# First attention of a macaron block pair: side work in smaller pieces per slot, and score products on 64-row halves with two key copies

## What is computed

```python
    def _L0_attn_ref(x, Wq, bq, Wk, bk, Wv, bv, Wo, bo):
        ...
        q = x @ Wq + bq
        k = x @ Wk + bk
        v = x @ Wv + bv
        ...
        scores = jnp.einsum('bghnd,bhsd->bghns', q, k)
        attn = jax.nn.softmax(scores / SCALE, axis=-1)
        out = jnp.einsum('bghns,bhsd->bghnd', attn, v)
        out = out.transpose(0, 3, 1, 2, 4).reshape(B, N, NUM_HEADS * HEAD_DIM)
        return out @ Wo + bo
...
    x = x + 0.5 * _L0_ffn_ref(_layernorm(x, axis=-1), ...)
    x = x + _L0_attn_ref(_layernorm(x, axis=-1), ...)
    x = x + 0.5 * _L0_ffn_ref(_layernorm(x, axis=-1), ...)
```

## Time and profile before

| | us |
|---|---|
| median of three runs | 1548.53 |
| profiled execution | 1547.1 |
| its span | 1545.2 |
| PE busy (matmul) | 1458.9 |
| DVE busy | 1103.2 |
| ACT busy | 956.2 |
| POOL busy | 581.6 |

### The profile page before, as it was taken

The page is one execution under the profiler, slowest core; times in us unless marked ns, Lnnn a source line. Parts: engine busy times, 40 slices in busy tenths (PEclk is TensorE's granted clock), DMA queues, the critical chain, the costliest instruction groups (busy, mean ns, idle before and its releaser), DMA issues.

```text
span 1545.2 us, 27899 instructions
## 1 busy us (share of the span) xinstructions
PE 1458.9 (94%) x9950; PEld 1189.4 (77%) x9950; DVE 1103.2 (71%) x2377; ACT 956.2 (62%) x1710; POOL 581.6 (38%) x551
## 2 busy tenths in 40 slices
PE   6999999889999999899999998999989999989998
PEld 6788888765555555488888887799977777769998
DVE  4766766777888888466766765477768888866765
ACT  6455555446666666655555556577736666658886
POOL 4466666500000000006666664477720111126664
PEclk9999999999999999999999998899999999999999
DMA  6000000000000000000000004000000000000000
GB/s 173 0 1 1 1 1 1 1 1 1 1 1 1 1 2 1 1 1 1 1 1 1 0 1 166 1 2 1 2 1 1 1 2 1 2 2 1 15 15 29
DMA packets 13320, 16.88 MB, mean 11 GB/s; under 512 B 768, under 2 KB 10496, under 8 KB 12928
## 3 DMA queue, kind: packets, MB, share of 16 engines
q1 hardware_dynamic: 13184, 15.11, 3.1%
HBM read 13.01 MB, written 2.10 MB: 10 GB/s over the span
## 4 chain that ended last, share of the span: by engine, by line
PE 78%; DVE 9%; ACT 8%; issue 4%; DMA 1%; POOL 0%; DVEq 0%; SPq 0%; POOLq 0%; ACTq 0%
PE PS L604 20%; PE PS L632 10%; PE PS L1738 9%; PE PS L1751 8%; PE PS L761 3%; PE PS L740 3%; PE PS L748 3%; ACT AR L855 2%; PE PS L718 2%; PE PS L1108 2%; PE PS L1112 2%; PE PS L1083 2%; PE PS L1065 1%; PE PS L1093 1%; PE PS L1132 1%
## 5 line engine op out<-in xcount | busy, mean ns | idle before, releaser
L542 POOL TENSOR_TENSOR RR<-AR,RR 128x512 fp32r<-128x512 f32 x150 | 193.9, 1293 | 516.1 <-ACT RR L565 516.1
L579 ACT ACTIVATE AR<-PS 128x512 f32<-128x512 f32 x224 | 134.0, 598 | 197.3 <-PE PS L604 196.1
L521 DVE TENSOR_TENSOR AR<-AR,PS 128x512 f32<-128x512 f32 x224 | 153.7, 686 | 132.4 <-PE PS L604 132.3
L855 ACT ACTIVATE AR<-PS 128x512 f32<-128x512 f32 x256 | 149.5, 600 | 98.1 <-PE PS L748 96.7
L924 DVE TENSOR_REDUCE AR<-PS 128x2 f32<-128x512 f32 x256 | 173.4, 686 | 47.3 <-PE PS L740 45.6
L604 PE MATMUL PS<-XHI,WG 128*128 128x512 f32 x448 | 175.8, 392 | 0.0
L604 PE MATMUL PS<-XHI,WU 128*128 128x512 f32 x448 | 174.6, 390 | 0.2
L525 DVE TENSOR_TENSOR AR<-AR,PS 128x512 f32<-128x512 f32 x224 | 153.8, 687 | 8.0 <-POOL RR L542 0.3
L1738 PE MATMUL PS<-XHI,SL 128*128 128x256 f32 x576 | 133.8, 287 | 2.5 <-DVE XTR L1904 1.4
L1738 PE MATMUL PS<-XLO,SL 128*128 128x256 f32 x576 | 133.0, 286 | 1.5 <-DVE XTR L1904 1.3
L1828 ACT ACTIVATE PS<-PS 128x1024 f32<-128x1024 f32 x96 | 96.8, 1009 | 55.1 <-PE PS L1738 54.9
(11 more groups left out here) (299 smaller groups left out, 3466.7 us busy)
## 6 DMA issues: line engine op xcount, KB each, us to landing
X<-in_x SPq DMA_DIRECT2D x4, 512.0 KB, 6.4
RAWZ<-in_zone_up SPq DMA_DIRECT2D x8, 256.0 KB, 4.8
RAWZ<-in_zone_down SPq DMA_DIRECT2D x8, 256.0 KB, 5.0
out_x<-X SPq DMA_DIRECT2D x4, 512.0 KB, 3.2
AR<-in_w SPq DMA_DIRECT2D x1, 1792.0 KB, 11.6
XT<-in_w SPq DMA_DIRECT2D x1, 1608.0 KB, 8.8
XT<-in_sel SPq DMA_DIRECT2D x1, 896.0 KB, 7.0
SM<-in_small SPq DMA_DIRECT2D x1, 857.5 KB, 6.8
```

Of the source, the lines that this page charges most:

```text
L521: v.tensor_tensor(PRD[:, m % 2, :], SIL[:, m % 2, :], bank(2 + m % 2), ALU.mult).then_inc(S.prod, 1)
L542: g.tensor_tensor(HL[k % 3], GAT[:, m % 2, :], HH[k % 3].bitcast(F32), ALU.subtract).then_inc(S.h_lo, 1)
L579: act.activation(SIL[:, m % 2, :], bank(m % 2), ACT.Silu).then_inc(S.silu, 1)
L855: act.activation(PT[:, g % 2, k, 2 * jp:2 * jp + 2, :], bank(2 + m % 2).rearrange("p (j q) -> p j q", j=2), ACT.Exp, scale=SC0).then_inc(S ...
```

## The change

*Key copies.* `KS0` keeps two copies (o = 0, 1). Copy o is zero on the groups g with g % 2 != o, by the new mask `ODD[:, o]` (sum of mask columns o and o + 2, made once). A score product takes only 64 partitions, `half_rows(h)`: 0 to 63 hold groups 0 and 1, 64 to 127 groups 2 and 3. `scores(b, m)` takes h = m // 4 % 2 and j = m % 4, both copies, so the second half of the queries is needed from place 2 on, not 4. `scores_t(b, m)` goes through the groups in the ORDER 0, 2, 1, 3. With the lead of 4, at any slot `scores` and `scores_t` are on different halves and in different banks. The address of the maxima and the layout of the outputs follow.

*Pieces.* `values` is called per half of the keys (k), four products each, in two adjacent slots; `queries` becomes `query`, one product per slot; `turn(i - 1, 1)` and `maxima` are halved over two slots; slots are dealt anew on PE (in the diff), ACT and DVE. On ACT `keys` goes from slots 0, 1 to 3, 4, `query` from 3 to 6 to 5, 6, 8, 9, and `rounded` from 7, 8 to 7, 10. On DVE `vals` goes from slot 2 to 4, `key_stacks` from 3, 4 to 5, 7, `normalise(i - 1, 1)` from 5 to 6, `stacks` from 8, 9 to 9, 13, and `normalise` of half 0 from slot 13 to slot 1 of the next step.

```diff
-            def queries(b, half):
-                if half:
+            def query(b, j):
+                half = j // 2
+                if j == 2:
                     pe.wait_ge(S.kx, b + 1)
                     pe.wait_ge(S.v, b + 1)
...
             def scores(b, m):
-                k, j, gp = m // 8, m // 2 % 4, m % 2
+                k, h, j = m // 8, m // 4 % 2, m % 4
...
-                if m in (0, 4):
-                    pe.wait_ge(S.qs, 2 * b + m // 4 + 1)
+                if m in (0, 2):
+                    pe.wait_ge(S.qs, 2 * b + m // 2 + 1)
                 wait(pe, S.smax, NS0 * b + m - 1)
-                pe.matmul(bank(m % 2), QS0[b % 3][:, j * SEQ + k * P:j * SEQ + (k + 1) * P], KS0[b % 3][:, 2 * gp:2 * gp + 2, :],
-                          start=True, stop=True).then_inc(S.s_pe, 1)
+                pe.matmul(bank(m % 2), QS0[b % 3][half_rows(h), j * SEQ + k * P:j * SEQ + (k + 1) * P],
+                          KS0[b % 3][half_rows(h), :, :], start=True, stop=True).then_inc(S.s_pe, 1)
...
-                g, k, jp = m // 4, m // 2 % 2, m % 2
-                pe.matmul(bank(2 + m % 2), KS0[b % 3][:, g, k * P:(k + 1) * P], QS0[b % 3][:, jp * 512:(jp + 1) * 512],
+                g, k, jp = ORDER[m // 4], m // 2 % 2, m % 2
+                rows = half_rows(g // 2)
+                pe.matmul(bank(2 + m % 2), KS0[b % 3][rows, g % 2, k * P:(k + 1) * P], QS0[b % 3][rows, jp * 512:(jp + 1) * 512],
                           start=True, stop=True).then_inc(S.st_pe, 1)
 
-            def values(b, g):
-                pe.wait_ge(S.exp, NS0 * b + 4 * g + 4)
+            def values(b, g, k):
+                pe.wait_ge(S.exp, NS0 * b + 4 * g + 2 * k + 2)
...
-                    if m == 0 and far:
+                    if m < 2 and done:
+                        values(i - 1, 3, m)
+                    if m == 2 and far:
                         key_value(i + 2)
-                    if m == 1 and done:
-                        values(i - 1, 3)
-                    if m == 1 and far:
-                        queries(i + 2, 0)
-                    if m == 3 and far:
-                        queries(i + 2, 1)
-                    if m == 4 and done:
-                        turn(i - 1, 1)
-                    if m in (5, 9) and now:
-                        values(i, m // 4 - 1)
-                    if m == 7 and done:
+                    if m in (3, 4) and far:
+                        query(i + 2, m - 3)
+                    if m in (4, 5) and done:
+                        turn(i - 1, 1, m - 4)
+                    if m in (5, 6) and now:
+                        values(i, 0, m - 5)
+                    if m in (6, 7) and far:
+                        query(i + 2, m - 4)
+                    if m == 8 and done:
                         back(i - 1)
-                    if m == 10 and done:
+                    if m in (9, 10) and now:
+                        values(i, 1, m - 9)
+                    if m == 11 and done:
                         project_out(i - 1)
                     if m == 12 and now:
-                        turn(i, 0)
-                    if m == 13 and next_:
-                        maxima(i + 1)
-                    if m == 13 and now:
-                        values(i, 2)
+                        turn(i, 0, 0)
+                        turn(i, 0, 1)
+                    if m in (13, 14) and next_:
+                        maxima(i + 1, m - 13)
+                    if m in (14, 15) and now:
+                        values(i, 2, m - 14)
...
-                for g in (2 * part, 2 * part + 1):
-                    last = v.tensor_scalar(KS0[b % 3][:, g, :], KSF0, T.masks[:, 2 + g:3 + g], None, ALU.mult)
+                ins = v.tensor_scalar(KS0[b % 3][:, part, :], KSF0, ODD[:, part:part + 1], None, ALU.mult)
```

More of the change, by code:

```diff
@@ L680, in program @@
         QH0 = XHI[:, 3072:4096]
-        KS0 = [XLO[:, u * 1024:(u + 1) * 1024].rearrange("p (g k) -> p g k", g=4) for u in range(3)]
+        KS0 = [XLO[:, u * 512:(u + 1) * 512].rearrange("p (o k) -> p o k", o=2) for u in range(3)]
         KH0 = XLO[:, 3072:3328]
@@ L711, in key_value, with maxima @@
                 last.then_inc(S.kv, 1)
-            def queries(b, half):
-                if half:
+            def query(b, j):
+                half = j // 2
+                if j == 2:
                     pe.wait_ge(S.kx, b + 1)
                     pe.wait_ge(S.v, b + 1)
[L717 to L722, removed]
+                ins = pe.matmul(bank(5 - half)[:, j % 2 * SEQ:(j % 2 + 1) * SEQ], T.wqs[:, j * P:(j + 1) * P], x_of(b),
+                                start=True, stop=True)
+                if j % 2:
+                    ins.then_inc(S.q, 1)
+            def maxima(b, half):
                 pe.wait_ge(S.mm, b + 1)
@@ L725, in maxima @@
                 for k in range(2):
-                    for j in range(4):
+                    for j in (2 * half, 2 * half + 1):
                         last = pe.transpose(bank(4, 2)[:, j * SEQ + k * P:j * SEQ + (k + 1) * P],
@@ L758, in values, with turn @@
                 o = bank(6 + g // 2)
[L759 to L765, removed]
-                pe.wait_ge(S.os, 2 * b + half + 1)
[L767 to L771, removed]
+                for j in range(4):
+                    last = pe.matmul(o[32 * j:32 * j + 32, g % 2 * SEQ:(g % 2 + 1) * SEQ], VA3[:, b % 3, k, ORDER[g], :],
+                                     PT[:, g % 2, k, j, :], start=(k == 0), stop=(k == 1), skip_group_check=True)
+                if k:
+                    last.then_inc(S.av, 1)
+            def turn(b, half, k):
+                pe.wait_ge(S.os, 2 * b + half + 1)
+                for g in range(2):
+                    at = half * 512 + g * SEQ + k * P
+                    last = pe.transpose(bank(6 + half)[:, (k * 2 + g) * P:(k * 2 + g + 1) * P], OS[:, at:at + P], ident)
+                if k:
+                    last.then_inc(S.ot, 1)
             def back(b):
@@ L893, in a0_dve @@
             rchain, mchain, kchain = Chain(v, S.r_chain), Chain(v, S.m_chain), Chain(v, S.k_chain)
+            kchain.link(v.tensor_tensor(ODD, T.masks[:, 2:4], T.masks[:, 4:6], ALU.add))
             def vals(b):
@@ L928, in maxima @@
                 v.wait_ge(S.smax, NS0 * (b + 1))
-                wait(v, S.mt, b)
+                wait(v, S.mt, 2 * b)
                 if b == 0:
@@ L969, in step @@
                         smax(b, s)
-                    if m == 2 and far:
+                    if m == 1 and done:
+                        normalise(i - 1, 0)
+                    if m == 4 and far:
                         vals(i + 2)
-                    if m in (3, 4) and far:
-                        key_stacks(i + 2, m - 3)
-                    if m == 5 and done:
+                    if m in (5, 7) and far:
+                        key_stacks(i + 2, m // 7)
+                    if m == 6 and done:
                         normalise(i - 1, 1)
-                    if m in (8, 9) and far:
-                        stacks(i + 2, m - 8)
+                    if m == 9 and far:
+                        stacks(i + 2, 0)
                     if m == 11 and next_:
@@ L981, in step @@
                         add(i - 1)
-                    if m == 13 and now:
-                        normalise(i, 0)
+                    if m == 13 and far:
+                        stacks(i + 2, 1)
                     if m in (14, 15) and next_:
```

35 lines of the change are left out of this document (22 added, 13 removed).

## The result

The changed kernel takes 1574.1 us (four runs, 1571.6 to 1576.5) against 1547.7 before; the ratio is 1.0171 with a 95% interval of 1.0147 to 1.0195. It is slower by 1.7%. I had forecast 1533.5 and the range 1515 to 1565, so the sign and the range are wrong. The profiled execution took 1576.5 us, with a span of 1574.6, 29.4 us more than before.

The account below looks back on a forecast made before the run. PE was taken to bound the first attention, with 17.1 us of work and 3.3 of waits per 20.44 us step. A new step of 18.6 + 0.6 = 19.2 us gave -15 us in all: 1533.5 us, range 1515 to 1565.

Parts of the forecast that it names:

- PE's floor before and after: PE's own work in one step of the first attention: 17.1 us before the change, 18.6 us after.
- the price of a pair (0.43): Two score products on opposite halves: load 0.10, one stream 0.23, drain 0.10, so 0.43 us against 0.46 before.
- half a block (0.57): Half a block of values on PE: 0.57 us, 1.00 less two groups of 0.22, eight a step.
- a change of the array's division by rows as by columns: Switching PE between row halves and other tilings costs the same as by columns: 0.19 against 0.20 us.
- the two rivals on concurrency: Score pairs: halves not streaming together (0.66 us, total 1576, chance 0.14), or only weight loads in a row (0.54, 1549, 0.15).
- The waits of `key_value` and of the second queries: PE's waits for DVE's shifts (slot 0) and the values' bias (slot 3) both go: -1.55 us a step.
- DVE's fewer key copies: Two of four masked copies go, 0.6 us of DVE a step; worth nothing on the path.
- part (a): Fewer waits in a step: two go, -1.55 us; a slot-by-slot walk found 0.3 left, 0.6 taken.
- The waits move: Rival: DVE's reduce-shift chain or ACT in slots 8 to 10 holds PE as long as now; 1569 at worst, chance 0.14.
- the sum (e): Step 19.2 us: thirteen steps -16, start +1.6, first and last but one -0.5 each, last +0.5; together -15 us.
- the rival without concurrency: The halves of a score pair do not stream together: pair 0.66 us, +27 us, total 1576, chance 0.14.
- part (c): Opposite halves: a pair of score products streams together on PE and costs 0.43 us against 0.46 before.

Follow-up runs that it names:

- e4: The changed kernel with the second half of the query stacks on DVE in slot 12, ahead of the addition, not slot 13: 1526.3 us, ratio 0.9853.
- e10: e8 with three keep-busy products instead of one after each score product in the start: 1588.7 us, one execution.
- e5: The changed kernel with full 128-row score products, four key copies and the second query stack in slot 12: 1526.8 us, ratio 0.9869 against the kernel before.
- e1: The changed kernel with full 128-row score products and four key copies again, keeping the new dealing of slots: 1547.0 us, ratio 1.0001 against the kernel before.
- e7: The changed kernel with five full keep-busy products inside PE's wait for the second query stack, from the third batch on: 1563.6 us, ratio 1.0112.
- e2: The kernel before with only the halves (two key copies, 64-row products, new group order), old dealing of slots: 1567 to 1600 us in four runs.
- e6: e4 with the start's full keep-busy product replaced by a second 64-row product on the opposite half, in 20 slots: 1537.5 us, ratio 0.9936.
- e8: e4 with both score products of each slot on the same 64 rows: 1585.0 us, ratio 1.0274; two more executions took 1834.3 and 1835.7 us.
- e9: e4 with 128-row products from own key copies for the first pass of batch 0 and second pass of batch 15: 1520.5 us, ratio 0.9828.

## Why the prediction was wrong

*Right.* PE's floor before and after, the price of a pair (0.43), of half a block (0.57), of a change of the array's division by rows as by columns, and the two rivals on concurrency as not true: e4's step is 18.64 for a floor of 18.6, e10's 21.95 for 22.2. The waits of `key_value` and of the second queries went as said. That DVE's fewer key copies were worth nothing on the path fits e5, where DVE waits 0.39 us for PE between its four copies and the second half of the stacks; no run took the copies alone.

*Wrong, first:* the step that failed in the waits is part (a), the walk through the new step. I took DVE's chain of slots 12 to 15 with the stacks in slot 13 and compared its end with what waits for the two shifts. I did not ask who waits for the stacks themselves. The diff has it: `if m in (0, 2)`, where it was `(0, 4)`, and place 2 stands in slot 14. The wait of 1.5 to 1.7 us made the waits of a step 1.25 us where I took 0.6; 13 x 0.65 = 8 us, and a forecast of 1542 with all else as it was. The rival "The waits move" (0.14) was nearest in kind, but it looked at the shifts and at ACT. e4 shows the cause: with the stacks one slot earlier the step is 18.64.

*Wrong, second and larger:* in the sum (e), a cost put at nothing without a reason. Every stretch was taken at the clock of before. The earlier trace rows showed 1.00 and I read it as given. The change put half-array products in the place of full ones and left an idle wait between them; then the clock fell, at the start for 47.8 us, in the steps and at the end. The start alone was +16.6 where (e) had +1.6, the first full step +5.1 for -0.5, the last +5.7 for +0.5, and the low stretches of the thirteen steps were 10.2 where the sum had none. That the time is near the 1576 of the rival without concurrency is chance: its mechanism is refuted by the starts of the pairs.

*Wrong, and of no weight:* two of the signs. The product behind a pair was to start some 0.33 us after it; by part (c) itself it is 0.43, and that was measured. ACT's wait for L755 was to fall well below 5.8 us; it was 6.2 (500 to 520 us), and 5.0 in the step of e4.

*What stays open.* Which property of PE's work lets the clock fall was not separated. Full products with the same wait kept it (e1), and in the changed kernel the low stretches of the steps went when the wait was taken away (e4) or filled (e7). But the wait is not needed: halves lost the clock in e2 with no wait over 0.84 us, in e6 in a last step that kept it in e4, and in e4's own start. Pairs on both halves in the start lost it too (e6), so neither the missing half nor the drains alone explain it. Where the low stretches begin differs between executions (e4, e8).

## What to carry to other kernels

When a change makes matmuls smaller or makes TensorE wait, check the granted clock stretch by stretch before and after, and price a stall with the clock that it may cost: here one stall of 1.5 to 1.7 us a step was worth 48 us. When an operation is moved and its consumer is moved too, look for the new consumer of each moved result, by name, not only for those that waited before. Here halves of the array gave 0.5 us a step where both were busy (e4 against e5); where one stood alone, at the ends of the pipeline, full products were the better choice (e9 against e4). When a small difference hangs on the clock, look at several executions: one kernel here took 1585 or 1835 us.

## What was new of the hardware

Products on opposite 64-row halves start within 0.003 to 0.004 us of each other in most pairs (232 of 256 in the changed kernel) and take the time of one; their weight loads start together as well. A pair stood 0.43 us before the next piece in another division, against 0.66 on one half.

The lower level of the clock can last under full load: in the profiled execution of e8 the granted clock was 0.50 for 621 us with PE busy 99.9% of it, and three other executions of the same kernel took 1584 to 1594 us, over 240 less. A step was 38.9 us there and 21.95 in e10.

A wait of 1.5 to 1.7 us once in 20 us was followed by a fall of the clock in about half of the steps with half-array products (changed kernel), and in none with full ones (e1).
